# Another order of the score and maximum steps in a two-layer attention and mixture-of-experts kernel

## The reference, cut to what matters

```python
q = jnp.einsum('ntc,hdc->nhtd', x_q, w_q)      # 16 heads of 64
k = jnp.einsum('ntc,hdc->nhtd', x_q, w_k)
v = jnp.einsum('ntc,hdc->nhtd', x_q, w_v)
a = jnp.einsum('nhtd,nhsd->nhts', q, k) / math.sqrt(q.shape[3])
causal_forbidden = jnp.arange(t)[:, None] < jnp.arange(t)[None, :]
a = jnp.where(causal_forbidden[None, None], -jnp.inf, a)
a = jax.nn.softmax(a, axis=3)
y = jnp.einsum('nhts,nhsd->nthd', a, v).reshape(a.shape[0], t, -1)
return y @ w_o
```

## Time and profile before

| | |
|---|---|
| median of 3 runs | 2139.63 us (2139.45 to 2143.38) |
| the profiled execution | 2139.86 us, of which the span is 2138.1 us |
| granted TensorE clock, mean | 0.986 |
| PE, DVE, POOL, ACT busy | 95%, 69%, 64%, 45% of the span |
| the 31 row phases with maximum steps | start from 638.95 to 1644.74 us |

### The profile page before, as it was taken

The page is one execution under the profiler, slowest core; times in us unless marked ns, Lnnn a source line. Parts: engine busy times, 40 slices in busy tenths (PEclk is TensorE's granted clock), DMA queues, the critical chain, the costliest instruction groups (busy, mean ns, idle before and its releaser), DMA issues.

```text
span 2138.1 us, 35690 instructions
## 1 busy us (share of the span) xinstructions
PE 2027.5 (95%) x13542; PEld 1601.3 (75%) x13542; DVE 1484.7 (69%) x3189; ACT 966.0 (45%) x1559; POOL 1374.5 (64%) x1238
## 2 busy tenths in 40 slices
PE   7998999999999999999999998899899899999998
PEld 5445888889787776877668775677676588899997
DVE  7375688686648877567876678885978546975554
ACT  6212553444335555435554354552455335444443
POOL 4313676677528877647777476673678937777774
PEclk9999999999999999999999999999999999999999
DMA  4533544555431001012010111101100245545552
GB/s 138 187 104 104 140 124 111 139 130 162 93 99 31 21 26 45 11 41 80 21 50 11 40 63 38 36 26 40 50 11 1 87 139 142 122 117 126 138 146 33
DMA packets 133788, 172.32 MB, mean 81 GB/s; under 512 B 16873, under 2 KB 109041, under 8 KB 133617
## 3 DMA queue, kind: packets, MB, share of 16 engines
q1 hardware_dynamic: 109040, 136.47, 19.9%
q0 software_dynamic: 24576, 33.57, 9.4%
HBM read 130.03 MB, written 39.85 MB: 79 GB/s over the span
## 4 chain that ended last, share of the span: by engine, by line
PE 57%; DVE 14%; POOL 10%; issue 7%; ACT 2%; DMA 1%; SPq 1%; POOLq 0%; DVEq 0%; ACTq 0%
PE psum L1425 13%; PE psum L1446 11%; PE psum L1573 7%; POOL t_acc L2655 7%; PE psum L1595 7%; PE psum L1633 5%; PE psum L1496 5%; PE psum L1510 3%; DVE t_mx L2401 2%; PE psum L1534 2%; DVE f_hhi L2336 2%; DVE psum L2370 2%; DVE f_hlo L2338 1%; POOL t_p L2635 1%; DVE t_turned L2442 1%
## 5 line engine op out<-in xcount | busy, mean ns | idle before, releaser
L2655 POOL TENSOR_TENSOR t_acc<-t_acc,t_p 128x1024 f32<-128x1024 f32 (+2 forms) x254 | 418.1, 1651 | 21.0
L1898 ACT ACTIVATE t_p<-psum 128x1024 f32<-128x1024 f32 (+2 forms) x291 | 292.0, 1018 | 95.7 <-PE psum L1573 85.4
L2572 POOL TENSOR_TENSOR f_wlo<-f_wst,f_whi 128x256 fp32r<-128x256 f32 x256 | 221.9, 943 | 167.8 <-ACT f_whi L1826 167.8
L1446 PE MATMUL psum<-f_whi,f_hhi 128*128 128x256 f32 x992 | 286.4, 289 | 7.8 <-DVE f_hlo L2338 7.7
L2336 DVE CAST f_hhi<-f_h 128x512 fp32r<-128x512 f32 x256 | 141.8, 554 | 212.1 <-ACT f_h L1846 211.5
L1846 ACT ACTIVATE f_h<-psum 128x512 f32<-128x512 f32 x256 | 153.1, 599 | 282.4 <-PE psum L1425 270.2
L1446 PE MATMUL psum<-f_whi,f_hlo 128*128 128x256 f32 x992 | 280.4, 283 | 0.0
L1446 PE MATMUL psum<-f_wlo,f_hhi 128*128 128x256 f32 x992 | 280.2, 282 | 0.0
L1595 PE MATMUL psum<-t_p,t_v 128*64 128x512 f32 (+3 forms) x1536 | 256.8, 491 | 3.3 <-ACT t_neg L1909 2.1
L1595 PEld LDWEIGHTS psum<-t_p,t_v 128*64 128x64 f32 x1536 | 105.7, 138 | 148.5 <-issue 133.9
L1425 PE MATMUL psum<-f_xhi,f_whi 128*128 128x512 f32 x512 | 205.5, 401 | 7.0 <-DVE f_xlo L2322 3.8
(11 more groups left out here) (315 smaller groups left out, 4782.1 us busy)
## 6 DMA issues: line engine op xcount, KB each, us to landing
f_wst<-in_L_ffn_w SPq DMA_DIRECT2D x64, 1024.0 KB, 5.7
t_wk<-wkT SPq DMA_DIRECT2D x32, 256.0 KB, 3.8
t_wq<-wqT SPq DMA_DIRECT2D x32, 256.0 KB, 2.8
t_wv<-wvT SPq DMA_DIRECT2D x16, 512.0 KB, 3.7
normal<-f_xy SPq DMA_DIRECT2D x5, 1024.0 KB, 5.4
a_x<-in_L_attn_a_x SPq DMA_DIRECT2D x4, 1024.0 KB, 7.8
res<-a_x SPq DMA_DIRECT2D x32, 128.0 KB, 2.7
t_xy<-res SPq DMA_DIRECT2D x4, 1024.0 KB, 6.1
```

The source lines that it names most:

```text
L1446: m = pe.matmul(out, h[:, js], w[:, f, :], start=(f == 0 and a == 0 and j % 2 == 0), stop=(f == FT - 1 and a == 2), skip_group_check=True)
L1898: act.activation(t["group"][group], k.bank_pair[odd // 2][:, :, 0:k.group_width(group)], ACT.Exp, scale=1.0 / float(np.sqrt(k.DH))).then_i ...
L2572: m = pool.tensor_tensor(t["wlo"][n % 2][:, i, ks], t["wst"][:, i, ks], t["whi"][n % 2][:, i, ks].bitcast(F32), ALU.subtract)
L2655: pool.tensor_tensor(acc[:, :, q0:], (p0 if kt == 1 else acc)[:, :, q0:], p[:], ALU.add).then_inc(k.p_acc, 1)
```

## The change

The table of the row phase has another order and other bank pairs. The score steps keep their order among themselves; the maximum steps do not. The phase begins with S00 in place of M40; M40, which was first, is third from the end; after the last score step stand three maximum steps (M40, M51, M61) where one stood (M30). The list of single banks goes 6, 7, 4, 5, 2, 3, 0, 1. `FIRST_MAX` only finds the first maximum step for a wait that was tied to the first entry. No instruction is added or taken away; behind line 29 the line numbers grow by one.

```diff
-    ("max", ((4, 0),), 1), ("score", ((0, 0),), 2), ("max", ((5, 0),), 3), ("score", ((0, 1), (0, 3)), 0),
...
+    ("score", ((0, 0),), 0), ("max", ((7, 0),), 1), ("score", ((0, 1), (0, 3)), 2), ("max", ((6, 0),), 3),
...
+FIRST_MAX = next(group for what, group, _ in ROW_STEPS if what == "max")
@@ -1070,7 +1071,7 @@
-            self.work_ring = [6, 7] + 6 * [2, 3, 0, 1, 4, 5]
+            self.work_ring = [6, 7] + 6 * [4, 5, 2, 3, 0, 1]
@@ -2388,7 +2389,7 @@
-        if group == ROW_STEPS[0][1]:
+        if group == FIRST_MAX:
```

More of the change, by code:

```diff
@@ L23 @@
 ROW_STEPS = (
-    ("max", ((4, 0),), 1), ("score", ((0, 0),), 2), ("max", ((5, 0),), 3), ("score", ((0, 1), (0, 3)), 0),
[L25 to L28, removed]
+    ("score", ((0, 0),), 0), ("max", ((7, 0),), 1), ("score", ((0, 1), (0, 3)), 2), ("max", ((6, 0),), 3),
+    ("score", ((1, 0),), 0), ("max", ((3, 0),), 1), ("score", ((1, 1),), 2), ("max", ((7, 1),), 3),
+    ("score", ((0, 2), (1, 6)), 0), ("max", ((5, 0),), 1), ("score", ((1, 2),), 2), ("score", ((1, 3),), 3),
+    ("max", ((2, 0), (0, 0)), 0), ("score", ((1, 4),), 1), ("score", ((1, 5), (1, 7)), 2), ("max", ((4, 0),), 3),
+    ("max", ((5, 1), (1, 0)), 1), ("max", ((6, 1), (4, 1)), 0),
 )
+FIRST_MAX = next(group for what, group, _ in ROW_STEPS if what == "max")
 LAST_STEPS = tuple(("score", ((c, kt),), (4 * c + kt + 1) % 4) for c in range(2) for kt in range(4 * (c + 1)))
```

## The result

The changed kernel took 2160.56 us (median of 4 runs, 2158.02 to 2163.88), the kernel before 2139.93 us beside it (4 runs): ratio 1.0094, 95% interval 1.0076 to 1.0112. It is slower, by 20.6 us; forecast were 2161.0 us. The total fits better than its terms do: the largest cost came out 7 us smaller, the gain at the head 4 us larger, and 14.5 us came from a place that the forecast had priced at 2.

A forecast was written before the change was run, and what follows sets the result against it. PE, busy 95% of the span, was taken to bound the kernel. 26.7 - 9.9 + 3.5 + 0.7 + 3.0 - 0.9 - 1.7 = +21.4 us on 2139.86 gives 2161 us; 8-in-10 range 2147 to 2172.

The forecast's parts named there:

- The end of the phase: End of the row phase: PE waits 0.89 us for bank 7 ahead of the projections in thirty units, +26.7 us.
- the middle: Middle of the row phase: new order as tight as the old; nothing, upper bound 0.15 us a unit, 4 us.
- The rival "no change": PE waits only 0.3 to 0.5 us at the row phase's end; about 2140 to 2147 us, chance 0.10.
- The head: Start of the row phase: DVE may come 0.94 us later; eleven late units get back about 0.9 each, -9.9 us.
- The clock and the tail in units 6 and 14: Behind these row phases: PE waits longer for t_xTlo, 2 x 1.2 us; the clock falls, +3.0 us net.
- DVE's tail elsewhere: DVE's maxima end later: absorbed in normal units, about 1.1 us in unit 22, +0.7 us for e_wide.
- The rival that DVE's lateness goes on: DVE's later end reaches the den and value products in every unit, 30 x 0.4 us more, 2173; chance 0.12.
- The ends: Ends of the attention: unit 0's wait for unit 1's projections goes, -0.9 us; unit 30's wait at L1393, -1.7 us.

The follow-up runs named there:

- the run with the head alone: Kernel before with M40 and S00 exchanged at the start of the row phase; ratio 1.0055, 2151.7 us at 2139.93.
- the exchanged pair: Changed kernel with M40 ahead of S15 in place of behind it; ratio 0.9928 to the kernel before, 2124.5 us.
- the last experiment: Changed kernel with DVE's TENSOR_SCALAR t_xy as 255 elements, read as 3 rows of 85, written as 5 of 51, plus one element; ratio 1.0115.

## Why the prediction was right

*The end of the phase, +26.7.* The mechanism and its place are shown, by five runs with waits of 0, 0.25, 0.4, 0.78 and 1.78 us, in which unit 4 takes 28.27, 28.45, 28.55, 28.99 and 30.80 us. The wait was 0.78 us in place of 0.89: the chain of 1.77 us was forecast to 0.01, but the three steps take 0.99 us of it, which I had at 0.89. Beyond that, the phase without its wait is 11.37 us (12.15 less 0.78) where the old one was 11.50. The difference is the stop of 0.14 us ahead of S14 in the old order, which is gone: the middle, put at nothing with a bound of +4, was a gain of 4. The rival "no change" had named such small waits near S14 and S15; they were real, but too small for it. Net 0.65 a unit, 19.5 in all, 7 less than forecast.

*The head, -9.9.* Measured -14.1 in eleven units: ten of the forecast's, and unit 13, which has waits of other kinds; the forecast's eleventh, unit 30, stands under the ends. I capped each at 0.94, one score step; units 1, 21 and 22, where DVE is 2 to 3 us late, got back 2.1 to 2.3 each. The new middle has slack as well, and the run with the head alone, which waits about 0.4 us in twenty more units, shows that S00 in front does not bring it without that middle.

*The clock and the tail in units 6 and 14, +5.4 (two thirds of the tail's 3.5, and 3.0).* Measured +5.4: PE waits 0.79 ahead of the transposes and 2.51 behind them in unit 6, in place of 1.00 behind them alone, and the granted clock of the unit is 0.95 in place of 1.00. The fall of the clock, for which I had left a lower bound of nothing, came. That the sum is met to 0.1 us is luck: the wait for t_xTlo grew by 1.5 us a unit in place of 1.2, the wait for t_parts stayed (0.57 and 0.92 us) where I had it vanish, and what is left for the clock is 1.3 to 1.5 us a unit (my estimate, by difference) in place of 2.4.

*DVE's tail elsewhere, +1.1 in unit 22 and +0.7 for e_wide.* This step failed. I wrote that in a normal unit the 2 us by which DVE ends later are absorbed, and looked only for what follows in DVE's list; I took its durations from the earlier trace rows as fixed. In units 10, 12, 18, 23 and 24 a small instruction of DVE stands there that POOL's additions can hold; about 16 us into the unit, where the new order puts it, it meets the start of one and lasts 1.7 to 2.5 us in place of 0.2 to 1.6. These units are 8.4 us longer behind their row phases; 5.3 of that is the longer duration of the instruction itself, the other 3.1 that DVE comes to it later. In units 1, 21, 22 and 25 such an instruction was held for about 2 us already, and DVE now comes to it 0.7 to 1.4 us later, counted from the end of the row phase: 5.4 us, of which 1.1 in unit 22, as forecast, and about 1.7 by the fallen clock of unit 21 (0.95). Unit 20 is 0.8 us longer, but not by a wait of this kind: the 0.7 for e_wide did not come, PE waits 5.7 us for it before and after, and the clock at half speed now falls on other work behind it. With 0.1 less in the rest that is 14.5 us in place of 1.8. Half the reduction, the exchanged pair and the split additions each take most of it away. The rival that DVE's lateness goes on had the right object, and nearly half of these 14.5 us are that lateness; but it is not in every unit, it is not t_parts, and it needs the held instruction to come through.

*The ends, -0.9 and -1.7.* Unit 30's row phase is 3.35 us shorter: its wait ahead of L1393 falls from 1.73 to 0.36, and 1.8 us of waits ahead of maximum steps go too, where I had counted nothing beyond 0.9 for a late head. The attention starts 3.4 us earlier. But the versions with M40 ahead of S15 and with half of its reduction start at 639.48 and 639.91 with the same head, no earlier than the kernel before (638.95), so the forecast's 0.9 is not shown and I hold the 3.4 for scatter.

Sum as measured: 19.5 - 14.1 + 5.4 + 14.5 - 3.35 + 0.35 (unit 0, 2 and 16) - 3.4 + 0.8 = 19.7. The wait was forecast 7.2 us too high, the head 4.2 and the ends 3.0 too high, the tail 12.7 too low: the total was right partly by luck, the 3.4 us of scatter included. The direction was not luck, since the wait alone is more than all the gains forecast.

The rule of the Trainium skill, "Perfetto Trace Analysis", section Matmuls, that groups which go round the banks hide their evacuation, holds here only if what follows outlasts matmul start, evacuation and hand-over, 1.77 us against about 1.0. What the Trainium skill, "TensorE: Matmul & The Clock Gate", says on its second failure mode was not seen in the changed kernel: with a stop of 0.78 us in each of thirty units a normal unit's clock is 1.00, and the mean is 0.985 against 0.986. With stops of 1.8 us, in the kernel before with another list of banks, the clock was 0.95 in seven units that had 1.00 before.

## What to carry to other kernels

A bank that is wanted again needs work behind its last user for as long as the whole chain of first matmul, evacuation and hand-over; here that was 1.77 us, and the step itself with two short ones behind it (about 1.0 us) fell 0.78 short in each of thirty units. Moving the one long step between them (S15, 1.1 us) turned a loss of 0.9% into a gain of 0.7%. And a duration in a profile is one at its present moment: when a change shifts an engine's list against another's, look up the same instruction's shortest and longest duration, and what ran on the neighbour in the long ones.

## What the hardware showed that I had not expected

DVE instructions of 0.2 to 0.4 us took up to 2.5 us while POOL added tiles, and ended with POOL's addition: the custom operation on e_turned 0.19 or 1.98 us, the TENSOR_SCALAR on 256 columns 0.40 or 2.50, one on 8 columns 0.17 or 1.71. With POOL's additions halved the longest in the first two groups were 1.12 and 1.39. In the attention of the two kernels 24 instructions on t_xy, t_rstd and e_turned lasted over 1.5 us, and every one ended 0.03 to 0.16 us behind the end of an addition of POOL. The Trainium skill, "SBUF — State Buffer", section "Who interferes with whom", says that DVE and GpSimd share a pair of ports as an exclusive lock, that a DVE instruction with two SBUF inputs or in a two-port mode takes it, and that who comes second is fully blocked. The traces agree in their numbers: it is these kinds that were held, while the 62 TENSOR_REDUCEs of L2447, with one SBUF input each, all take 1219 to 1221 ns. No view names the mode of an instruction. A hint, by an estimate from the shortest durations of the last experiment: 255 columns of TENSOR_SCALAR took 396 ns and one column 258, which is 0.54 ns a column, where M40's reduction got 1.04 ns shorter for each column that half of it left out (1226 and 694 ns).
